# A one-core attention block: weight work moved out of the head, and a row of maxima written by eight one-column transfers

## The chip, the core and the metric

The kernel runs on one core of a Trainium2 chip. The metric is the device time of one launch in microseconds (us). Of three runs shown before the change, the median is 3070.46 us (3069.53 to 3070.96). The profile is one further execution.

## What is computed

Sixteen batches of 1024 tokens by 256 features go through an attention block and a small feed-forward block, both scaled and gated by values that come from a vector per batch. Cut to what matters here:

```
mod = silu(c) @ wmod                      # 16 x (6 * 256): sa, ca, ga, sb, cb, gb
ga, gb = sign(g) * max(|g|, 0.25)
h = layernorm(x) * (1 + ca) + sa
q = h @ Wq.T ; k, v = (h @ Wkv_down.T) @ Wk_up.T, ... @ Wv_up.T     # 8 heads of 64
x = x + ga * (softmax(q k^T / 8) v) @ Wo.T
h = layernorm(x) * (1 + cb) + sb
x = x + gb * (h @ weight.T + pooled(h) @ disha)
```

## The kernel before

All engines run one program written out by hand in slots. A slot is one batch's attention; its 64 steps are eight groups of eight. One group is half of the queries (512) of a pair of heads, so 1024 rows of scores; one step is one tile of 128 keys. Slot -1 is the head of the program: no attention yet, only what batch 0 needs. Slot 0 is batch 0's attention, and so on; the side work of the batches before and after is spread over a slot's steps.

In a step, TensorE (PE) makes the scores of one key tile in `scores()` (lines L668 and L670, two matmuls for each half), ScalarE (ACT) takes their exponential (L872), and GpSimd (POOL) adds the result to a running sum (L1043). In every fourth step PE multiplies four steps' probabilities with the values in `mix()` (L647). In every odd step `maximum()` makes plain scores for a later batch or group (L696), and VectorE (DVE) takes their maxima over the keys, negated, into two columns of `neg_max` (L1197). PE then does the step's side work (`side_work()`): projections L633, transposes L714, L729 and L769, out projection L762, feed-forward L781, sums for the denominators L748.

The maximum of each query row enters the scores as one more row of the product: row 127 of `query_m`. So a group's maxima, which DVE leaves as eight columns of 128 partitions, must be written as one row of 1024 numbers on one partition before the group's first score. The kernel before does that in three moves for each of 128 groups: PE turns the 128x8 block (L738), ACT copies the 8x128 result to `max_row` (L980), and one transfer of eight pieces of 512 bytes writes the row (L566). The first score of a group waits for it in `scores()`, at the group's step 0:

```
if k == 0:
    need(pe, max_row_set, 16 * (GROUPS * z.c + g + 1))
```

All transfers of the kernel are issued by SyncE (SP) in program order. For the group after the one under way SP issues, at steps counted in the group: copies of the queries (L558 to L560, step 1, after the last score of the group before), the spread of the denominators (four transfers L574, step 2), the reciprocals to a scratch in memory (L580, step 3), and back (two transfers L586, step 4), then the row of maxima (L566, step 6). At single steps of a slot there are also the load of the gates (L531, step 21), of the next batch (L522 and L527, steps 22 and 47), a row of ones (L547, step 30), and loads and stores of the residual.

The head (slot -1) starts with folding the weights, then normalizes and projects batch 0. The tables `FIRST` and `FOLDS` set the steps of what runs once: the gates (`gate`, L794 on PE, then `make_gates` on POOL), the columns of the second modulation (`mod_out`, the helper at L606), the transposed out weights (`wo_t`, L788), their four folds (`wo_fold`, L807) and `weight_t`. A step number of 64 or more (`STEPS + n`) means step n of slot 0. The row and the group work of batch 0 need eight queries' projections (`query`).

## Time and profile before

| | |
|---|---|
| median of three runs | 3070.46 us |
| profiled execution | 3068.32 us |
| its span in the trace | 3065.3 us |
| granted clock of TensorE, mean | 0.996 |
| PE busy | 3014.4 us, 98% of the span |
| POOL busy | 2544.3 us, 83% |
| DVE busy | 2146.2 us, 70% |
| ACT busy | 1720.2 us, 56% |
| queue of SP's transfers (q1) | 17.8% of 16 engines' span |

Busy time is the union of an engine's instructions; the profile says itself that matmuls are pipelined and that their ends are modelled, so a busy PE is not PE at its peak. The execution's own time is 3.0 us longer than its span. PE is busy in all slices of the span but the first, and the chain that ended last runs over PE for 94%.

### The profile page before, as it was taken

The page shows a single profiled execution, that of the slowest core. Times are in us where ns is not written, and L with a number is a line of the kernel's source. Part 1 is how long each engine was busy: PE and PEld are TensorE (multiplying, and loading weights), DVE is VectorE, ACT ScalarE, POOL GpSimd, SP SyncE. Part 2 cuts the span into 40 slices and gives each one's busy share as a digit, 9 for nine tenths or more (in the row PEclk, how much of TensorE's full clock was granted, in tenths as well). Part 3 has the DMA queues.
Part 4 walks back from the last instruction along what each step waited for, and adds up shares of the span by engine and source line. Part 5 has one row for each costly group of instructions (what it writes and reads, how often), then busy time and mean ns, then how long its engine had stood idle before and what let it go on. Part 6 is the DMA issues. An engine that isn't in the chain of part 4 may idle for free.

```text
span 3065.3 us, 45400 instructions
## 1 busy us (share of the span) xinstructions
PE 3014.4 (98%) x15394; PEld 1696.1 (55%) x15394; DVE 2146.2 (70%) x2548; ACT 1720.2 (56%) x3209; POOL 2544.3 (83%) x1520
## 2 busy tenths in 40 slices
PE   6999999999999999999999999999999999999998
PEld 4445555555555555555555555555555555555545
DVE  5466767767677676777767677676776767667665
ACT  3555555555555555555555555555555555555544
POOL 2788888888888888888888888888888888888796
PEclk9999999999999999999999999999999999999999
DMA  3111121121111111121211211211121111111111
GB/s 86 39 52 44 51 62 53 50 59 53 53 47 59 56 49 53 56 60 46 60 46 53 63 50 50 61 52 53 49 64 49 49 54 55 60 39 53 46 48 47
DMA packets 165621, 162.93 MB, mean 53 GB/s; under 512 B 62224, under 2 KB 113552, under 8 KB 165392
## 3 DMA queue, kind: packets, MB, share of 16 engines
q1 hardware_dynamic: 165392, 160.05, 17.8%
q8 instruction: 123, 2.02, 0.3%
q14 instruction: 106, 0.87, 0.1%
HBM read 74.40 MB, written 17.33 MB: 30 GB/s over the span
## 4 chain that ended last, share of the span: by engine, by line
PE 94%; DVE 2%; POOL 2%; DMA 1%; ACT 1%; issue 1%; SPq 0%; ACTq 0%; DVEq 0%; POOLq 0%
PE ps_mix L647 29%; PE ps_score L668 18%; PE ps_score L670 15%; PE ps_max L696 11%; PE ps_side L633 7%; PE ps_side L762 5%; PE ps_side L781 3%; PE ps_side L748 2%; POOL prob_sum L1043 1%; PE ps_side L714 1%; PE ps_side L738 1%; PE ps_side L769 1%; ACT probs L872 1%; DMA query_m<-max_row 0%; DVE neg_max L1197 0%
## 5 line engine op out<-in xcount | busy, mean ns | idle before, releaser
L1043 POOL TENSOR_TENSOR prob_sum<-prob_sum,probs 128x1024 f32<-128x1024 f32 x768 | 1861.1, 2423 | 352.8 <-ACT probs L872 275.8
L1197 DVE TENSOR_REDUCE neg_max<-ps_max 128x1 f32<-128x1024 f32 x1024 | 1204.3, 1218 | 310.9 <-PE ps_max L696 306.9
L872 ACT ACTIVATE probs<-ps_score 128x512 f32<-128x512 f32 x2048 | 1113.3, 597 | 474.0 <-PE ps_score L670 448.8
L647 PE MATMUL ps_mix<-probs,values 128*64 128x512 f32 x4096 | 935.4, 598 | 0.8 <-ACT probs L872 0.8
L668 PE MATMUL ps_score<-query,key_hi 128*128 128x512 f32 x2048 | 881.0, 430 | 9.4 <-ACT probs L872 7.9
L670 PE MATMUL ps_score<-query_m,key_lo 128*128 128x512 f32 x2048 | 809.5, 395 | 0.0
L647 PEld LDWEIGHTS ps_mix<-probs,values 128*64 128x64 f32 x4096 | 271.3, 136 | 532.8 <-issue 531.6
L668 PEld LDWEIGHTS ps_score<-query,key_hi 128*128 128x128 f32 x2048 | 384.7, 188 | 260.5 <-ACT probs L872 100.8
L670 PEld LDWEIGHTS ps_score<-query_m,key_lo 128*128 128x128 f32 x2048 | 386.7, 189 | 45.2
L696 PE MATMUL ps_max<-key_hi,query 64*128 64x512 f32 x2048 | 376.2, 445 | 3.7 <-DVE neg_max L1197 3.7
L1043 POOL TENSOR_TENSOR prob_sum<-probs 128x1024 f32<-128x1024 f32 x128 | 311.6, 2434 | 56.4 <-ACT probs L872 56.4
L909 ACT ACTIVATE mixed<-ps_mix 128x512 f32<-128x512 f32 x128 | 76.4, 597 | 327.1 <-PE ps_mix L647 327.1
L696 PEld LDWEIGHTS ps_max<-key_hi,query 64*128 64x128 f32 x2048 | 152.9, 185 | 188.5 <-issue 164.7
L980 ACT ACTIVATE max_row<-ps_side 8x128 fp32r<-8x128 f32 x127 | 33.9, 267 | 371.4 <-PE ps_side L738 371.4
L1163 DVE TENSOR_TENSOR mixed<-mixed,recip 128x512 f32<-128x512 f32 x127 | 172.2, 1356 | 97.5 <-DMA recip<-recip_scratch 96.1
L1240 DVE TENSOR_TENSOR query<-ps_side,query 64x512 fp32r<-64x512 f32 x252 | 173.6, 689 | 56.7 <-ACT query L919 52.5
L919 ACT ACTIVATE query<-ps_side 64x512 fp32r<-64x512 f32 x252 | 149.1, 592 | 78.5 <-PE ps_side L633 75.5
L1270 DVE TENSOR_TENSOR x_mid<-ps_side,x_mid 128x256 f32<-128x256 f32 x121 | 51.0, 422 | 195.2 <-PE ps_side L762 195.2
L762 PE MATMUL ps_side<-w_out_hi,mixed_lo 128*128 128x256 f32 x480 | 134.5, 280 | 0.0
L762 PE MATMUL ps_side<-w_out_lo,mixed_hi 128*128 128x256 f32 x480 | 134.5, 280 | 0.0
L762 PE MATMUL ps_side<-w_out_hi,mixed_hi 128*128 128x256 f32 x480 | 133.9, 279 | 0.0
L633 PE MATMUL ps_side<-h_hi,w_in_hi 128*128 128x512 f32 x314 | 127.1, 405 | 2.4 <-DVE query L1240 2.2
(203 smaller groups left out, 2860.0 us busy)
## 6 DMA issues: line engine op xcount, KB each, us to landing
query_m<-query SPq DMA_DIRECT2D x128, 256.0 KB, 2.5
query_m<-query SPq DMA_DIRECT2D x256, 128.0 KB, 2.6
recip<-recip_scratch SPq DMA_DIRECT2D x254, 128.0 KB, 2.9
x_in<-in_L_attn_x_dram SPq DMA_DIRECT2D x32, 512.0 KB, 4.8
x_mid<-in_L_attn_x_dram SPq DMA_DIRECT2D x64, 256.0 KB, 3.2
out_dram<-x_mid SPq DMA_DIRECT2D x64, 256.0 KB, 2.2
denoms<-recip SPq DMA_DIRECT2D x508, 1.0 KB, 1.7
gates<-gates_scratch SPq DMA_DIRECT2D x16, 256.0 KB, 4.5
```

The lines of the kernel that those rows point to most:

```text
L633: last = nc.tensor.matmul(side[:, :], w[:, f, rows], h[:, f, cols], start=(j == 0), stop=(j == len(products) - 1))
L647: last = nc.tensor.matmul(ps_mix[j * R:j * R + R, :], values[par][:, k, :], probs[:, (STEPS * z.c + s) % RING, j * HALF:(j + 1) * HALF], s ...
L668: nc.tensor.matmul(ps_score[j], key_hi[z.par][:, k * P:(k + 1) * P], group_queries(g)[:, j, :], start=True, stop=False)
L670: nc.tensor.matmul(ps_score[j], key_lo[z.par][:, k * P:(k + 1) * P], query_m[:, g % 2, j * HALF:(j + 1) * HALF], start=False, stop=True).t ...
L696: last = nc.tensor.matmul(ps_max[j][:, half * HALF:(half + 1) * HALF], query[rows, 2 * p + j, qt * P:(qt + 1) * P], key_hi[kpar][rows, hal ...
L762: last = nc.tensor.matmul(side[:, 0:D], mp[:, p, j * P:(j + 1) * P], wp[:, pair, :], start=(q == 0), stop=(q == len(products) - 1))
L872: nc.scalar.activation(probs[:, (STEPS * z.c + s) % RING, half * HALF:(half + 1) * HALF], ps_score[half], ACT.Exp, scale=SCALE).then_inc(e ...
L919: nc.scalar.activation(query[j * R:(j + 1) * R, 2 * p + j, half * HALF:(half + 1) * HALF], side[j * R:(j + 1) * R, :], ACT.Copy).then_inc( ...
L1043: nc.gpsimd.tensor_tensor(out=total[:, :], in0=before, in1=probs[:, now % RING, :], op=ALU.add).then_inc(adds_done, 1)
L1163: nc.vector.tensor_tensor(raw, raw, recip[:, :], ALU.mult).then_inc(group_mixed, 1)
L1197: nc.vector.tensor_reduce(neg_max[:, col:col + 1], ps_max[j][:, :], AX_X, ALU.max, negate=True).then_inc(maxima_done, 1)
L1240: last = nc.vector.tensor_tensor(query[(1 - j) * R:(2 - j) * R, 2 * p + j, cols], side[j * R:(j + 1) * R, :], query[j * R:(j + 1) * R, 2 * ...
```

## The change

Two parts. In the first, `wo_t`, `mod_out` and the first `wo_fold` leave slot -1 for steps 10 to 34 of slot 0, and the other folds and `weight_t` move later; the gates stay in slot -1 but are made in two halves at steps 54 and 56; one query projection goes from slot -1 to slot 0. The weights are loaded into other places so that they can live longer, and DVE takes the statistics of both halves of batch 0 before it copies the folded weights. In the second, `max_row` is gone: SP writes row 127 of `query_m` from `neg_max` itself, by eight transfers of one column of 128 numbers each, one step earlier in its program.

```
@@ tables
 FIRST = {
-    "query": (7, 58, 62, 63, STEPS, STEPS + 2, STEPS + 4, STEPS + 6),
+    "query": (7, 60, 62, STEPS, STEPS + 1, STEPS + 2, STEPS + 4, STEPS + 6),
     "values_t": (11, 12),
-    "wo_t": (54, 56),
-    "gate": (56,),
-    "max_row": (60,) + tuple(STEPS - NT + 5 + NT * i for i in range(1, GROUPS)),
-    "mod_out": (61,),
-    "wo_fold": (61, STEPS + 18, STEPS + 10, STEPS + 22),
-    "weight_t": (STEPS + 26, STEPS + 30),
+    "gate": (54, 56),
+    "mod_out": (STEPS + 10,),
+    "wo_t": (STEPS + 14, STEPS + 18),
+    "wo_fold": (STEPS + 22, STEPS + 26, STEPS + 30, STEPS + 34),
+    "weight_t": (STEPS + 36, STEPS + 38),
 }
@@ SP
-            sp.dma_start(s_wmod[:, :, 2 * D:], wmod_v[:, :, 2 * D:]).then_inc(wmod_rest_loaded, 16)
+            for j, part in enumerate((2, 5)):
+                sp.dma_start(s_wgate[:, :, j * D:(j + 1) * D], wmod_v[:, :, part * D:(part + 1) * D]).then_inc(wgate_loaded, 16)
+            sp.dma_start(s_wmod_out, wmod_v[:, :, 3 * D:5 * D]).then_inc(wmod_rest_loaded, 16)
...
-                        copy, row = STEPS + NT * (j - 1) + 1, step_of("max_row", j) + 1
+                        copy, row = STEPS + NT * (j - 1) + 1, STEPS + NT * (j - 1) + 5
...
-                            drained(sp, z, "max_row", j, need_alone)
+                            need_alone(sp, maxima_done, STEPS * b + NT * (j + 1))
                             need_alone(sp, query_m_copied, 48 * (GROUPS * b + j + 1))
-                            need_alone(sp, max_row_set, 16 * (GROUPS * b + j))
-                            sp.dma_start(query_m[P - 1:P, j % 2, :].bitcast(F32),
-                                         max_row[j % 2][:, :].bitcast(F32)).then_inc(max_row_set, 16)
+                            need_alone(sp, max_row_set, 16 * NT * (GROUPS * b + j))
+                            for u in range(NT):
+                                sp.dma_start(query_m[P - 1:P, j % 2, u * P:(u + 1) * P].bitcast(F32),
+                                             neg_max[:, NT * j + u:NT * j + u + 1].bitcast(F32),
+                                             allow_slow_non_contiguous=True).then_inc(max_row_set, 16)
@@ PE
-                        need(pe, max_row_set, 16 * (GROUPS * z.c + g + 1))
+                        need(pe, max_row_set, 16 * NT * (GROUPS * z.c + g + 1))
...
-                    elif kind == "max_row":
-                        need(pe, maxima_done, STEPS * b + NT * (i + 1))
-                        need(pe, side_drained[room], count)
-                        last = nc.tensor.transpose(side[0:NT, 0:P], neg_max[:, NT * i:NT * (i + 1)], ident[:, :])
@@ ACT
-                        elif kind == "max_row":
-                            need(act, side_full[room], count + 1)
-                            need(act, max_row_set, 16 * (GROUPS * b + i - 1))
-                            nc.scalar.activation(max_row[i % 2][:, :], side[0:NT, 0:P], ACT.Copy).then_inc(side_drained[room], 1)
@@ DVE
-            for i in range(NT // 2):
-                statistics(0, ORDER_0[0], i)
+            for part in ORDER_0:
+                for i in range(NT // 2):
+                    statistics(0, part, i)
             dve.wait_ge(fold_a, 1)
...
-            for i in range(NT // 2):
-                statistics(0, ORDER_0[1], i)
```

SP's program in the steady part, slot by slot the same. The place is slot 1, steps 26 to 33, before the change (L574, L580 and L586 carry the denominators, L566 the row of maxima, L558 to L560 the next group's queries):

```order
L574 DMA denoms<-recip 32x1x8 x4
L580 DMA recip_scratch<-denoms_r 128x8
L586 DMA recip<-recip_scratch 64x512 x2
L547 DMA key_lo<-ones_row 1x8x128
L566 DMA query_m<-max_row 1x8x128
L591 DMA out_dram<-x_mid 128x2x256
L558 DMA query_m<-query 128x512
L559 DMA query_m<-query 64x512
L560 DMA query_m<-query 64x512
```

and with the change, steps 20 to 30 of the same slot, from the reciprocals (now L591) and the load of the gates (now L534) on:

```order
L591 DMA recip<-recip_scratch 64x512 x2
L534 DMA gates<-gates_scratch 128x512
L570 DMA query_m<-neg_max 1x128x1 x8
L525 DMA x_in<-in_L0_attn_x_dram 128x4x256
L561 DMA query_m<-query 128x512
L562 DMA query_m<-query 64x512
L563 DMA query_m<-query 64x512
L579 DMA denoms<-recip 32x1x8 x4
L585 DMA recip_scratch<-denoms_r 128x8
L591 DMA recip<-recip_scratch 64x512 x2
L570 DMA query_m<-neg_max 1x128x1 x8
L550 DMA key_lo<-ones_row 1x8x128
```

Where one transfer stood, eight stand; the load of the next batch and the row of ones, which stood ahead of the row, now stand behind it, and the load of the gates still stands ahead.

PE's program in the head, from the first group's scores for maxima on (L696; the first group's are the first four sets), before:

```order
L696 MATMUL ps_max<-key_hi,query 128x512 x4
L788 MATMUL ps_mix<-ident,probs 128x128 x4
L696 MATMUL ps_max<-key_hi,query 128x512 x4
L788 MATMUL ps_score<-ident,probs 128x128 x4
L794 MATMUL ps_score<-probs,mixed 16x256 x4
L696 MATMUL ps_max<-key_hi,query 128x512 x4
L633 MATMUL ps_side<-h_hi,w_in_hi 128x512
```

and, after that query's projection (L633), the end of the first group's maxima:

```order
L696 MATMUL ps_max<-key_hi,query 128x512 x4
L738 MATMUL ps_mix<-ident,neg_max 8x128
L696 MATMUL ps_max<-key_hi,query 128x512 x4
L606 MATMUL ps_score<-mixed,probs 128x16 x8
L807 MATMUL ps_score<-mixed 64x256 x2
```

With the change, from the same place to the first projection (L701 is the old L696, L795 the old L794, L638 the old L633):

```order
L701 MATMUL ps_max<-key_hi,query 128x512 x4
L795 MATMUL ps_mix<-probs,mixed 16x256 x2
L701 MATMUL ps_max<-key_hi,query 128x512 x4
L795 MATMUL ps_score<-probs,mixed 16x256 x2
L701 MATMUL ps_max<-key_hi,query 128x512 x8
L638 MATMUL ps_score<-h_hi,w_in_hi 128x512
```

Between the first group's four sets of scores only the two halves of the gates are left, and the query's projection stands behind all four; the transposes, the modulation (L606) and the fold (L807) are gone from the head.

## Rows read from the trace of the kernel before

**Rows 1.** The page: the chain that ended last, shares by engine.

```profile
PE 94%; DVE 2%; POOL 2%; DMA 1%; ACT 1%; issue 1%; SPq 0%; ACTq 0%; DVEq 0%; POOLq 0%
```

**Rows 2.** Timeline, 1512 to 1528 us: start, duration, engine, line, operation, count.

```profile
1512.50 2.46 SPq L574 DMA_DIRECT2D denoms<-recip  x4
...
1516.10 2.36 DVE L1197 TENSOR_REDUCE neg_max<-ps_max 128x1 f32<-128x1024 f32 x2 [0.90 <-PE ps_max L696]
...
1520.14 1.14 SPq L586 DMA_DIRECT2D recip<-recip_scratch  x2
...
1524.41 0.72 SPq L566 DMA_DIRECT2D query_m<-max_row  x1
...
1527.80 0.50 PE L668 MATMUL ps_score<-query,key_hi 128*128 128x512 f32 x1
```

**Rows 3.** Timeline of SP and PE, two later groups, 1591 to 1620 us.

```profile
1591.30 1.13 SPq L586 DMA_DIRECT2D recip<-recip_scratch  x2
...
1598.14 0.50 PE L668 MATMUL ps_score<-query,key_hi 128*128 128x512 f32 x1
...
1614.28 0.52 SPq L531 DMA_DIRECT2D gates<-gates_scratch  x1
...
1619.95 0.50 PE L668 MATMUL ps_score<-query,key_hi 128*128 128x512 f32 x1
```

**Rows 4.** Timeline of SP, one of the late groups, 752 to 761 us.

```profile
756.04 1.13 SPq L586 DMA_DIRECT2D recip<-recip_scratch  x2
...
760.52 0.53 SPq L558 DMA_DIRECT2D query_m<-query  x1
```

**Rows 5.** Sources: single instructions, ns min/median/max, first and last start.

```profile
L738 PE MATMUL ps_side<-ident,neg_max x127: 272/273/273, 79.7 to 3005.4; 128*8 128x128 f32 x127
...
L574 SPq DMA_DIRECT2D denoms<-recip x508: 523/591/1683, 98.7 to 3018.6; - x170
...
L558 SPq DMA_DIRECT2D query_m<-query x128: 492/516/545, 34.9 to 2987.1; - x128
...
L566 SPq DMA_DIRECT2D query_m<-max_row x128: 670/720/744, 49.8 to 3006.1; - x128
...
L515 SPq DMA_DIRECT2D gates_scratch<-x_mid x4: 412/420/424, 81.2 to 82.6; - x4
```

**Rows 6.** The page: issues by line, KB each, median us from issue to landing.

```profile
query_m<-query SPq DMA_DIRECT2D x128, 256.0 KB, 2.5
...
denoms<-recip SPq DMA_DIRECT2D x508, 1.0 KB, 1.7
...
gates_scratch<-x_mid SPq DMA_DIRECT2D x4, 8.0 KB, 1.4
mixed<-in_L_c_dram SPq DMA_DIRECT2D x2, 8.0 KB, 3.4
```

**Rows 7.** Timeline of PE, end of a `mix()`: with L738 behind it.

```profile
1499.27 1.89 PE L647 MATMUL ps_mix<-probs,values 128*64 128x512 f32 x8
1501.09 0.27 PE L738 MATMUL ps_side<-ident,neg_max 128*8 128x128 f32 x1
...
1501.43 0.40 PE L670 MATMUL ps_score<-query_m,key_lo 128*128 128x512 f32 x1
```

**Rows 8.** The same in the last batch, where no L738 stands.

```profile
3023.81 1.89 PE L647 MATMUL ps_mix<-probs,values 128*64 128x512 f32 x8
...
3025.97 0.40 PE L670 MATMUL ps_score<-query_m,key_lo 128*128 128x512 f32 x1
```

**Rows 9.** Timeline of PE and POOL in the head and slot 0; brackets: idle before, what ended it.

```profile
24.67 1.97 PE L714 MATMUL ps_score<-ident,x_in 128*128 128x128 f32 x8 [4.27 <-POOL x_in L1011]
...
34.29 0.65 PE L788 MATMUL ps_mix<-ident,probs 128*128 128x128 f32 x4
...
38.15 3.46 PE L794 MATMUL ps_score<-probs,mixed 128*16 128x256 f32 x8
...
50.42 3.59 PE L606 MATMUL ps_score<-mixed,probs 128*128 128x16 f32 x16
...
53.95 1.97 PE L807 MATMUL ps_score<-mixed 64*64 64x256 f32 x4
...
60.76 0.39 PE L668 MATMUL ps_score<-query,key_hi 128*128 128x512 f32 x1
...
71.64 0.24 POOL L997 TENSOR_SCALAR rstd<-moments 128x4 f32<-128x4 f32 x1 [20.78 <-DVE moments L1112]
...
97.12 1.08 PE L748 MATMUL ps_side<-prob_sum,ones_cols 128*32 128x256 f32 x8 [3.88 <-POOL prob_sum L1043]
```

**Rows 10.** Windows: us, busy (x count) of PE, PEld, DVE, ACT, POOL, granted clock, DMA share, GB/s.

```profile
50.00:60.00 10.00, 10.00 (x37) 7.00 (x34) 2.71 (x5) 1.77 (x3) 0.86 (x3) 0.58 0.18 53
```

More of the change, by code:

```diff
@@ L306, in adaln_block @@
         query_m = sb("query_m", [P, 2, T], F32R)
-        neg_max = sb("neg_max", [P, STEPS])
-        max_row = [sb(f"max_row{i}", [NT, P], F32R) for i in range(2)]
+        neg_max = sb("neg_max", [P, STEPS], F32R)
         probs = sb("probs", [P, RING, T])
@@ L341, in adaln_block @@
         s_disha = stage[1][:, 2304:2560]
[L342 to L344 removed]
+        s_c = stage[1][:, 5120:5120 + NF * B].rearrange("p (k b) -> p k b", k=NF)
+        s_silu = stage[1][:, 5152:5152 + 3 * NF * B].rearrange("p (j k b) -> p j k b", j=3, k=NF)
+        s_wo_t = stage[1][:, 3712:4736].rearrange("p (k n) -> p k n", k=PAIRS)
         s_w_in = probs[:, 0:2, 0:H * R + P]
@@ L419, in adaln_block @@
         wmod_rest_loaded = sem("wmod_rest_loaded")
+        wgate_loaded = sem("wgate_loaded")
         qk_loaded = sem("qk_loaded")
@@ L599, in _, with modulate @@
         def _(pe):
-            def modulate(bank, parts):
-                for j, part in enumerate(parts):
+            def modulate(bank, weight):
+                for j, part in enumerate((1, 0)):
                     for f in range(NF):
@@ L606, in modulate @@
                             last = nc.tensor.matmul(bank[:, (2 * j + f) * B:(2 * j + f + 1) * B],
-                                                    s_wmod[:, k, part * D + f * P:part * D + (f + 1) * P],
+                                                    weight[:, k, part * D + f * P:part * D + (f + 1) * P],
                                                     s_silu[:, 2, k, :], start=(k == 0), stop=(k == NF - 1))
@@ L789, in side_work @@
                     elif kind == "gate":
-                        pe.wait_ge(wmod_rest_loaded, 16)
+                        if i == 0:
+                            pe.wait_ge(wgate_loaded, 32)
                         need(pe, side_drained[room], count)
-                        for j, part in enumerate((2, 5)):
-                            for k in range(NF):
-                                last = nc.tensor.matmul(side[0:B, j * D:(j + 1) * D], s_silu[:, 2, k, :],
-                                                        s_wmod[:, k, part * D:(part + 1) * D], start=(k == 0), stop=(k == NF - 1))
+                        for k in range(NF):
+                            last = nc.tensor.matmul(side[0:B, 0:D], s_silu[:, 2, k, :], s_wgate[:, k, i * D:(i + 1) * D],
+                                                    start=(k == 0), stop=(k == NF - 1))
                     elif kind == "mod_out":
                         pe.wait_ge(side_drained[room], count)
-                        last = modulate(side, (4, 3))
+                        pe.wait_ge(wmod_rest_loaded, 16)
+                        last = modulate(side, s_wmod_out)
                     elif kind == "wo_fold":
@@ L967, in slot @@
                             need(act, side_full[room], count + 1)
-                            nc.scalar.activation(s_gate[2], side[0:B, :].rearrange("p (j n) -> p j n", j=2),
-                                                 ACT.Copy).then_inc(side_drained[room], 1)
+                            nc.scalar.activation(s_gate[2][:, i, :], side[0:B, 0:D], ACT.Copy).then_inc(side_drained[room], 1)
                         elif kind == "wo_fold":
@@ L1016, in make_gates @@
                 sign, size, raw = s_gate[0], s_gate[1], s_gate[2]
-                drained(pool, z, "gate", 0, need_alone)
+                for i in range(2):
+                    drained(pool, z, "gate", i, need_alone)
                 nc.gpsimd.tensor_scalar(sign, raw, 0.0, 2.0, ALU.is_ge, ALU.mult).then_inc(gate_steps, 1)
```

18 lines of the change are left out of this document (8 added, 10 removed).

## The prediction

> **What bounds the kernel now.** I read the chain of the page first, then the timeline around one group boundary, then SP's part of it over a batch, then the head. The chain runs over PE for 94% [rows 1], and the page has PE busy in every slice but the first: in slots 1 to 15 whatever delays PE is paid in full, and whatever another engine saves is worth nothing by itself. POOL, busy 83%, does not stop PE there. So three questions decide: what the removed transposes cost PE, whether the new transfers deliver the row of maxima before PE asks for it, and what the head gives.
>
> The reader should see in [rows 2] how late the row of maxima is made. SP's last duty before it is the pair of transfers L586, issued by 1520.14 + 1.14 = 1521.28. The group's maxima were complete at 1516.10 + 2.36 = 1518.46. The first score of the next group starts at 1527.80. I call the time between, 6.52 us, the window: the whole row must be issued and landed in it, because the new code lets SP go on as soon as the maxima are there, without waiting for PE and ACT. Before the change SP sat idle to 1524.41, issued once for 0.72, and the row was in time.
>
> **Part by part.**
>
> *The windows.* They repeat slot by slot, because both of their ends hang on PE's own fixed order. Groups of four places in a slot of eight have about 6.5 us. Three places have 5.7: 1591.30 + 1.13 = 1592.43 to 1598.14 [rows 3]. The place with the load of the gates has less, since that load still stands ahead of the row: 1614.28 + 0.52 = 1614.80 to 1619.95, 5.15 us. The load of the next batch and the row of ones, which shorten two places before, move behind the row and cost it nothing. In about 20 of the 126 groups of the steady part something came late, mostly the store of reciprocals; one of them is 756.04 + 1.13 = 757.17, the next group's copies starting at 760.52 just before its first score at about 761.0, a window of 3.8 [rows 4].
>
> *What the row needs.* Eight issues one after another and the landing of the last: about 0.1 to start, 7 times the distance of two issues, and one landing. No element-wise transfer inside the memory of the core is in the trace, so both are bounded by neighbours. The distance: L515 takes 0.42 to issue, which with a gap of 0.04 gives 0.46; L558, also 128 partitions, takes 0.516; L566, the old row, takes 0.72 [rows 5]. The nearest in kind is L574: small, inside the core's memory, between one partition and many, issued in a loop. Four of them take 2.46 [rows 2], the last 0.59, so a distance of (2.46 - 0.59) / 3 = 0.62. I take 0.62, with 0.46 and 0.76 as ends. The landing: 1.4 for L515, 1.7 for L574, 2.5 for the copies of queries, 3.4 for the load of `c`, which also goes number by number [rows 6]. I take 1.7, again L574's. Need: 0.1 + 7 x 0.62 + 1.7 = 6.14 us; ends 0.1 + 7 x 0.46 + 1.4 = 4.7 and 0.1 + 7 x 0.76 + 2.5 = 7.9.
>
> Why not the old row's 0.72, whose destination is the same partition? It has eight pieces and the new ones have 128 each, the count of L558, which is issued faster. The Trainium skill, DMA: Bandwidth & Descriptors, section "Why a DMA increments its semaphore by 16 and not by 1", says that a transfer whose slowest dimension is 8 uses 8 engines and SP then writes the missing increments itself, while 128 uses all 16. By that rule the 0.72 holds an extra that the new ones don't pay; with 0.76 as the distance instead, the sum below would be about 105 us higher.
>
> *What is missing is a stall of PE.* At a need of 6.14: the places with 6.5 stay free; some 37 regular groups with 5.7 lose 0.43 each, 16 us; some 14 with 5.15 lose 1.0, 14 us; about 21 late or odd groups lose 1.3 on average, 27 us. Sum **+57 us**. PE can't win this back: it is busy throughout and everything behind moves with it. The ends of the need give about +5 and, with a mean window of 5.85, 126 x 2.1 = +265.
>
> *The transposes.* 127 of L738 at 0.272 would be 34 us [rows 5], but they hide. With L738 between, L670 starts 0.27 after the end of the last `mix()` matmul (1501.43 against 1499.27 + 1.89) [rows 7]; in the last batch, where nothing stands between, also 0.27 (3025.97 against 3023.81 + 1.89) [rows 8]. The small matmul runs in the time in which PE changes from one tiling to the other. I take -1 us, with -34 as the far end. ACT's copy and its wait go too; ACT is no bound, and its exponentials wait for PE's scores anyway: nothing.
>
> *The head.* Two savings. The second half's statistics now run before the copies, so POOL normalizes it earlier; PE's idle 4.27 before L714 at 24.67 [rows 9] shrinks, ACT's chain behind it starts about 3 us earlier. Then the gates hold up the third set of scores for maxima in one piece of 3.46; the halves now fit into PE's waits for DVE. L788 (0.65, twice), L606 (3.59), L807 (1.97) and one projection (about 2.5 there) leave PE before the first score. That comes at 60.76 and should come near 49, then set by DVE's maxima and the row's transfers. POOL's next work waits for DVE's statistics of the next batch at 71.64 and paces PE to 97.12; both follow the first score, so about 11 us is won there. Given back in slot 0, where PE is the bound again after about 105: the transposes, the fold and part of the modulation, some 3 us at full clock; PE will also be idler in the head, and its granted clock, a mean of 0.58 between 50 and 60 us before (much of it at the lower level, 1.2 GHz) [rows 10], may cost part of the gain. I take **-8 us**, between -3 and -12. The loads have more issues (one more on SP ahead of the first row) and land long before steps 54 and 74: nothing. The later fold reaches POOL's gating at step 35 within a step of its wait; POOL has slack there and its ring of six steps covers PE: nothing, 2.5 at worst, once.
>
> *Sum.* The profiled execution took 3068.3: 3068.3 + 57 - 1 - 8 = 3116.3. The median of the runs shown lies 2.1 above it, so I forecast **3118 us**.
>
> **The rivals.**
>
> *The row fits.* If two issues lie 0.46 apart and land in 1.4, the need is 4.7 and only a handful of late groups stall, 5 us or less; what is left is the head. For it: SP is idle for 3 us in every window, and the new code starts earlier on purpose; single issues as short as 0.42 exist. Against it: none of the more than 1000 issues inside the core's memory is that short in the median. It decides below a need of about 5.1: 3070.5 - 1 - 8 + 3 = 3064, on the edge of what can be told, and if the transposes were on PE's path after all (against [rows 7, 8]) 3070.5 - 34 - 8 = 3028. This is the case on the other side of mine.
>
> *Numbers one by one are slow.* Each transfer writes 128 numbers of 4 bytes into one partition. The load of `c` is the only such pattern here and needs 3.4 to land [rows 6]. With 3.4 for 1.7 the need is 7.8, the stall 126 x 2.0 = 250, the time about 3310. For it: all 128 writes meet in one partition. Against it: that load has 2048 numbers per transfer, sixteen times as many, and comes from outside. The Trainium skill, DMA: Bandwidth & Descriptors, section "Rules for kernel authors", says not to transpose by a plain copy with a rearranged pattern and gives a factor of 19; it would make this rival the outcome. It speaks of bulk rate, and here 4 KB move in a window of microseconds, so I give it little.
>
> *The issue is as slow as the old row's.* With 0.76 apart and 1.7, the need is 7.1, and all places stall: 126 x (7.1 - 5.85), near 155, plus a little for the late groups, 3225.
>
> **How the numbers follow.** My forecast, a need between about 5.5 and 6.9, has 0.68 and gives 3082 to 3195. The row that fits has 0.19; of it 0.12 ends below 3064, 0.07 around 3067. Slow numbers 0.06, slow issues 0.07. The range reaches from 3066 to 3200: it leaves out the better part of the fitting row and the two slow cases, about 2 in 10. Faster or slower by 0.2% is about what a measurement of this kernel can tell from no change, 6 us: faster 0.12, within 0.08, slower 0.80.
>
> **What would show it.** In the profile after: eight issues per group on SP, 0.55 to 0.65 apart, starting right behind L586's successor instead of 3 us later; PE idle before the first score of a group, released by the transfer `query_m<-neg_max`, for some 60 to 80 of 128 groups, longest behind the load of the gates and zero at four places of the slot; PE's busy time lower by 34 but its span not; the first score near 49 us and the first denominators near 86. I would be wrong if that wait is absent (then distance or landing is shorter than any neighbour's), if it stands before all groups (then longer), or if PE's time from the last `mix()` to L670 falls by more than 0.05 per group.

## The result, and the profile after

The changed kernel takes **3241.03 us** (median of 4 runs, 3232.63 to 3255.41), the kernel before in the same sitting 3069.99: a ratio of 1.056, 95% interval 1.054 to 1.0579. It is slower by 171 us. I had forecast slower, but by 48 us, and the result lies above my range. The profiled execution took 3247.02 us, its span is 3245.2 (before 3065.3), its mean granted clock 0.983 (before 0.996).

The chain of the page, which ran over PE for 94% before [rows 1], now runs over PE for half; the rest is the row and what surrounds it. Page of the changed kernel, chain by engine and by line (L570 is the row, L673 and L675 the scores, L591 the reciprocals back, L585 their store):

```profile
PE 52%; SPq 19%; DMA 13%; issue 7%; DVE 6%; ACT 2%; POOL 1%; ACTq 0%; DVEq 0%; POOLq 0%
SPq L570 15%; PE ps_mix L652 15%; PE ps_score L673 11%; PE ps_score L675 8%; DMA query_m<-neg_max 7%; PE ps_max L701 6%; DMA recip_scratch<-denoms_r 5%; DVE neg_max L1191 5%; PE ps_side L638 4%; SPq L591 4%; PE ps_side L763 3%; PE ps_side L749 2%; PE ps_side L782 1%; POOL prob_sum L1039 1%; ACT probs L874 1%
```

Busy time on the page, and the two waits for the row (waits by engine and line: total, times, longest):

```profile
PE 3052.8 (94%) x15266; PEld 1720.0 (53%) x15266; DVE 2135.3 (66%) x2548; ACT 1688.6 (52%) x3082; POOL 2537.4 (78%) x1520
```

```profile
PE ps_score L673 <- DMA query_m<-neg_max: 143.7, 106, 3.2
...
PEld ps_score L673 <- DMA query_m<-neg_max: 200.1, 126, 3.6
...
DVE mixed L1157 <- DMA recip<-recip_scratch: 178.1, 111, 4.5
```

So the 179.9 us by which the span grew are two things. PE idles 3245.2 - 3052.8 = 192.4 us where it idled 50.9 before: +141.5. The waits for the row alone are 143.7 (PE itself waits in 106 of the 128 groups; its weight load, which stands ahead of the matmul, in 126). And PE is busy 38.4 us **more** (3052.8 against 3014.4), with 128 matmuls fewer. The granted clock says why. The lower level, 1.2 GHz, is half of the full one, so a mean of 0.983 means that (1 - 0.983) x 2 x 3245.2 = 110 us of the span ran at it.

One group, the place with the load of the gates; timeline of SP's queue and of PE in the changed kernel, answering [rows 3]:

```profile
1500.93 1.13 SPq L591 DMA_DIRECT2D recip<-recip_scratch  x2
1502.16 0.52 SPq L534 DMA_DIRECT2D gates<-gates_scratch  x1
1502.89 5.03 SPq L570 DMA_DIRECT2D query_m<-neg_max  x8
1508.07 0.48 SPq L525 DMA_DIRECT2D x_in<-in_L_attn_x_dram  x1
```

```profile
1509.39 0.80 PE L673 MATMUL ps_score<-query,key_hi 128*128 128x512 f32 x1 [2.99 <-DMA query_m<-neg_max]
...
1509.98 0.63 PE L675 MATMUL ps_score<-query_m,key_lo 128*128 128x512 f32 x1
...
1510.41 0.63 PE L673 MATMUL ps_score<-query,key_hi 128*128 128x512 f32 x1
```

The need can be read off whole. By the need I mean, as in the prediction, the time from the end of SP's last duty to the score. From 1502.16 + 0.52 = 1502.68 to 1509.39 are 6.71 us: 0.21 to the first issue, seven distances of (5.03 - 0.60) / 7 = 0.633, together 4.43 (0.60 is the median issue below), and 2.07 from the last issue to the score. The last part is 2.08 in the median of all groups that wait. Source and issues of the row, answering [rows 5] and [rows 6]:

```profile
L570 SPq DMA_DIRECT2D query_m<-neg_max x1024: 469/601/1661, 43.6 to 3187.0; - x171
```

```profile
query_m<-neg_max SPq DMA_DIRECT2D x1024, 0.5 KB, 2.2
...
denoms<-recip SPq DMA_DIRECT2D x508, 1.0 KB, 1.7
```

The same rows of PE show the second loss: after the idle 2.99 a score matmul takes 0.63 where it otherwise takes 0.40 [rows 7], and the first scores of the two halves start 1.02 apart (1509.39 and 1510.41). Windows of the changed kernel over that place (us, busy of PE, PEld, DVE, ACT, POOL, granted clock, DMA share, GB/s):

```profile
1502.00:1509.00 7.00, 4.40 (x26) 3.13 (x24) 4.27 (x7) 2.17 (x4) 6.57 (x4) 1.00 0.32 76
1509.50:1512.50 3.00, 3.00 (x7) 2.37 (x8) 1.35 (x2) 1.19 (x2) 0.73 (x1) 0.50 0.82 272
1513.00:1519.00 6.00, 6.00 (x35) 2.33 (x33) 2.95 (x3) 2.34 (x5) 2.36 (x1) 1.00 0.10 25
```

The clock falls to half behind the idle stretch, and PE does seven matmuls in 3 us, where at one each 0.23 us (1501.67, 1501.90 and 1502.13 in the kernel before) some thirteen fit. The span has 28 stretches at the lower level, against 4 before. Of the 28, 25 begin during or just after one of the 106 waits for the row: none at the 57 waits below 1.2 us, 25 at the 49 longer ones.

The next group shows the late kind, answering [rows 4] (timeline of SP and PE):

```profile
1526.01 0.33 SPq L585 DMA_DIRECT2D recip_scratch<-denoms_r  x1
...
1529.26 1.12 SPq L591 DMA_DIRECT2D recip<-recip_scratch  x2
...
1530.60 5.03 SPq L570 DMA_DIRECT2D query_m<-neg_max  x8
...
1537.10 0.50 PE L673 MATMUL ps_score<-query,key_hi 128*128 128x512 f32 x1 [1.92 <-DMA query_m<-neg_max]
```

SP may issue the reciprocals' way back (L591) only when their store (L585) has landed. From the one issue to the other are 3.25 us here and 1.47 in the median. I call a store late where it is over 2.5: that is so in 21 groups of the changed kernel and in 9 of the kernel before (counted over the trace). These 21 groups carry 50.6 us of the wait. In 16 others one of the eight issues of the row is slow (up to 1.66 us for 0.60), so that the last one starts more than 4.8 us behind the first instead of 4.43; they carry 19.2, and the remaining groups 73.9.

In the head the first score comes at 51.80 instead of 60.76 [rows 9].

### The profile page after: what moved, and what is told of

Read it like the earlier page. It is cut to its first block, busy times and chain, and to the rows that moved or that the text cites. A ratio compares the mean times of both kernels' runs of the same rounds, so it can differ in the third digit from the quotient of the medians.

```text
span 3245.2 us, 45663 instructions
## 1 busy us (share of the span) xinstructions
PE 3052.8 (94%) x15266; PEld 1720.0 (53%) x15266; DVE 2135.3 (66%) x2548; ACT 1688.6 (52%) x3082; POOL 2537.4 (78%) x1520
## 3 DMA queue, kind: packets, MB, share of 16 engines
q1 hardware_dynamic: 311344, 160.11, 19.2%
## 4 chain that ended last, share of the span: by engine, by line
PE 52%; SPq 19%; DMA 13%; issue 7%; DVE 6%; ACT 2%; POOL 1%; ACTq 0%; DVEq 0%; POOLq 0%
SPq L570 15%; PE ps_mix L652 15%; PE ps_score L673 11%; PE ps_score L675 8%; DMA query_m<-neg_max 7%; PE ps_max L701 6%; DMA recip_scratch<-denoms_r 5%; DVE neg_max L1191 5%; PE ps_side L638 4%; SPq L591 4%; PE ps_side L763 3%; PE ps_side L749 2%; PE ps_side L782 1%; POOL prob_sum L1039 1%; ACT probs L874 1%
## 5 line engine op out<-in xcount | busy, mean ns | idle before, releaser
L1191 DVE TENSOR_REDUCE neg_max<-ps_max 128x1 fp32r<-128x1024 f32 x1024 | 1204.1, 1217 | 326.9 <-PE ps_max L701 322.7
L673 PE MATMUL ps_score<-query,key_hi 128*128 128x512 f32 x2048 | 895.8, 437 | 151.7 <-DMA query_m<-neg_max 143.7
L675 PE MATMUL ps_score<-query_m,key_lo 128*128 128x512 f32 x2048 | 820.5, 401 | 0.0
L673 PEld LDWEIGHTS ps_score<-query,key_hi 128*128 128x128 f32 x2048 | 390.2, 191 | 511.5 <-DMA query_m<-neg_max 200.1
L1039 POOL TENSOR_TENSOR prob_sum<-probs 128x1024 f32<-128x1024 f32 x128 | 303.7, 2373 | 182.0 <-ACT probs L874 182.0
L675 PEld LDWEIGHTS ps_score<-query_m,key_lo 128*128 128x128 f32 x2048 | 393.1, 192 | 47.2
L701 PE MATMUL ps_max<-key_hi,query 64*128 64x512 f32 x2048 | 379.0, 448 | 8.9 <-DVE neg_max L1191 6.2
L701 PEld LDWEIGHTS ps_max<-key_hi,query 64*128 64x128 f32 x2048 | 154.4, 187 | 196.8 <-issue 180.4
L1264 DVE TENSOR_TENSOR x_mid<-ps_side,x_mid 128x256 f32<-128x256 f32 x121 | 50.9, 421 | 200.3 <-PE ps_side L763 200.3
L638 PE MATMUL ps_side<-h_hi,w_in_hi 128*128 128x512 f32 x314 | 132.8, 423 | 6.2 <-DVE query L1234 6.2
L638 PE MATMUL ps_side<-h_lo,w_in_hi 128*128 128x512 f32 x314 | 130.2, 415 | 0.0
```

Source lines behind the costliest of these rows:

```text
L638: last = nc.tensor.matmul(side[:, :], w[:, f, rows], h[:, f, cols], start=(j == 0), stop=(j == len(products) - 1))
L673: nc.tensor.matmul(ps_score[j], key_hi[z.par][:, k * P:(k + 1) * P], group_queries(g)[:, j, :], start=True, stop=False)
L675: nc.tensor.matmul(ps_score[j], key_lo[z.par][:, k * P:(k + 1) * P], query_m[:, g % 2, j * HALF:(j + 1) * HALF], start=False, stop=True).t ...
L701: last = nc.tensor.matmul(ps_max[j][:, half * HALF:(half + 1) * HALF], query[rows, 2 * p + j, qt * P:(qt + 1) * P], key_hi[kpar][rows, hal ...
L1039: nc.gpsimd.tensor_tensor(out=total[:, :], in0=before, in1=probs[:, now % RING, :], op=ALU.add).then_inc(adds_done, 1)
L1191: nc.vector.tensor_reduce(neg_max[:, col:col + 1], ps_max[j][:, :], AX_X, ALU.max, negate=True).then_inc(maxima_done, 1)
```

## The experiments

Each kernel was timed against the kernel before on the same chip. I call them e1 to e11, in the order in which they stand here.

### The head part alone

The changed tables, loads and statistics order, with the row as before:

```
-                            for u in range(NT):
-                                sp.dma_start(query_m[P - 1:P, j % 2, u * P:(u + 1) * P].bitcast(F32),
...
+                            sp.dma_start(query_m[P - 1:P, j % 2, :].bitcast(F32),
+                                         max_row[j % 2][:, :].bitcast(F32)).then_inc(max_row_set, 16)
```

> The first part of the change alone: gates, modulation and fold of the weights moved, statistics first; the row of maxima goes by transpose, copy and one transfer as before. Theory (the head is a gain, and the whole loss is PE waiting for the row): 3070 - 8 = 3062 us, between 3058 and 3067; PE's idle time before a group's first score stays below 3 us in all. Rival A (the work moved into slot 0, or the earlier start, is part of the loss): above 3075 us.

Measured: **3063.69 us** (10 runs, 3061.02 to 3068.4) against 3067.99; ratio 0.9987 (0.9978 to 0.9996). A gain of 4 us, about half of the 8 that I had in the sum. Timeline of PE, the first score and the first denominators, answering [rows 9]:

```profile
51.58 0.52 PE L674 MATMUL ps_score<-query,key_hi 128*128 128x512 f32 x1
...
92.82 0.64 PE L754 MATMUL ps_side<-prob_sum,ones_cols 128*32 128x256 f32 x8 [1.32 <-POOL prob_sum L1050]
```

The first score is 9.2 us earlier, the first denominators only 97.12 - 92.82 = 4.3, and that is what the span keeps (3060.8 against 3065.3). PE waits 3.6 us in all for the row, a little over the 3 that I had allowed.

### The row part alone

The same lines the other way round, in the kernel before: its tables and loads, with the eight transfers.

> The second part alone: eight transfers of one column for the row, the head as before. Theory: the changed kernel's 3241 plus the 8 us of the head that is not won: 3240 to 3260 us, PE's idle time before first scores about 145 us, the granted clock's mean about 0.98. Rival A: clearly below 3240, by what the head part would cost.

Measured: **3247.05 us** (3242.36 to 3256.78), ratio 1.0587 (1.0566 to 1.0607), clock 0.983. PE waits 147.9 us for the row. As expected: the whole loss is the row.

### Six of the eight columns at step 3

```
-                        if s == row % STEPS and there:
+                        if s in ((row - 2) % STEPS, row % STEPS) and there:
+                            early = s == (row - 2) % STEPS
...
-                            for u in range(NT):
+                            for u in (0, 1, 2, 4, 5, 6) if early else (3, 7):
```

> The changed kernel, but six of the eight columns, whose maxima are done two steps before, are sent between the spread of the denominators and the store of the reciprocals, where SP was idle; only two transfers are left behind the reciprocals' way back. Same number of transfers, same numbers, one order. Theory (the row's last issue and landing end after the window): the need falls from 0.2 + 7 x 0.63 + 2.1 = 6.7 to 0.2 + 0.63 + 2.1 = 2.9 us, less than any regular window, so the waits vanish and with them the low clock: 3061 us, between 3057 and 3072. Rival B (1024 transfers of single numbers slow the memory or the queue as such): still above 3150.

Measured: **3138.29 us** (3129.88 to 3141.64), ratio 1.0232 (1.0215 to 1.0249); the clock is 0.997. A miss: 60% of the loss goes, and a new wait comes. SP's queue in the timeline, and the waits of PE and DVE:

```profile
1516.67 2.49 SPq L580 DMA_DIRECT2D denoms<-recip  x4
1519.37 4.90 SPq L571 DMA_DIRECT2D query_m<-neg_max  x6
1524.42 0.49 SPq L586 DMA_DIRECT2D recip_scratch<-denoms_r  x1
1526.05 1.15 SPq L592 DMA_DIRECT2D recip<-recip_scratch  x2
1527.30 1.18 SPq L571 DMA_DIRECT2D query_m<-neg_max  x2
```

```profile
PE ps_max L702 <- DVE neg_max L1192: 52.7, 44, 2.5
PE ps_score L674 <- DMA query_m<-neg_max: 11.3, 20, 1.8
```

```profile
DVE mixed L1158 <- DMA recip<-recip_scratch: 310.0, 127, 6.3
```

The wait for the row fell from 143.7 to 11.3, so the row is in time when only two columns are late. But the six stand ahead of the store of the reciprocals (L586). They come back late, DVE waits 310 us for them instead of 96, its next maxima wait behind that on the same engine, and PE waits for DVE. What I had left out was the queue behind the inserted issues.

### The transpose issued twice, in the kernel before

```
+                        for _ in range(2):
-                        last = nc.tensor.transpose(side[0:NT, 0:P], neg_max[:, NT * i:NT * (i + 1)], ident[:, :])
+                            last = nc.tensor.transpose(side[0:NT, 0:P], neg_max[:, NT * i:NT * (i + 1)], ident[:, :])
```

> The kernel before with each of the 128 transposes of the maxima issued twice into the same place. Theory (the transpose hides in PE's change of tiling, so its removal gave nothing): if it is hidden wholly, the second adds at most its own 0.1 to 0.2 us where the first already fills the gap: 3070 to 3095 us, and the time from the last mix matmul to L670 shows how much of the first was hidden. Rival C (each transpose costs its 0.27 us): 3070 + 34 = 3104 us.

Measured: **3086.52 us** (3082.67 to 3089.6), ratio 1.0059 (1.0044 to 1.0074): by the ratio 18 us (14 to 23) for 128 more matmuls, 0.14 each. In the traces the score matmul L670 starts 0.976 us behind the start of the last `mix()` matmul, and 0.866 in the kernel before: 0.11 each. This doesn't say by itself what the first one costs; e9 does.

### PE kept busy in front of the wait

```
+                    if k == 0 and (z.c or g):
+                        need(pe, exps_done, 2 * (STEPS * z.c + s) - 1)
+                        for _ in range((1, 1, 3, 6, 1, 3, 3, 1)[g]):
+                            nc.tensor.matmul(ps_score[0], key_hi[z.par][:, k * P:(k + 1) * P],
+                                             group_queries(g)[:, 0, :], start=True, stop=True)
                     if k == 0:
```

> The changed kernel, with matmuls whose result is thrown away put in front of PE's wait for the row at every group's first score: 1, 1, 3, 6, 1, 3, 3, 1 of them by place in the slot, 0.4 us each, 19 in a slot, about as long as the median gap of each place in the changed kernel (0.34, 0.16, 0.96, 1.71, 0.30, 0.94, 0.95, 0.43). They add 19 x 0.4 x 16 = 122 us of PE's work, of which some 95 us stand in time that PE waited anyway. Theory A, TensorE's clock falls because PE sits idle at the group starts and that costs (110 - 30) / 2 = 40 us: the granted clock returns from 0.983 to 0.993 or more, PE's idle falls from 145 us to below 80, and the median is 3241 - 40 + 25 = 3226 (3205 to 3240). Rival B, the clock falls for another reason (the removed transposes, the transfers): the clock stays at 0.983 and the median is 3241 + 25 = 3266 (3250 to 3275).

Measured: **3221.1 us** (3212.89 to 3225.19), ratio 1.0496 (1.0475 to 1.0518), clock 0.993. PE does some 300 useless matmuls more than the changed kernel and is done 20 us sooner. That is theory A; rival B would be 3266. Its wait for the row is down from 143.7 to 50.2, and (1 - 0.993) x 2 x 3211.1 = 45 us are left at the lower clock instead of 110, a gain of 32. Not all of the time won need be the clock's: this trace has 14 late stores where the changed kernel has 21. What shows the cause is the granted clock itself, which rival B left at 0.983.

### The wait behind one more matmul

The second half's first product, which doesn't read the row, is issued before the wait instead of behind it; the two `key_lo` products follow together.

```
+                        if k > 0 or j == 1:
+                            if k == 0:
+                                need(pe, max_row_set, 16 * NT * (GROUPS * z.c + g + 1))
+                            for i in (0, 1) if k == 0 else (j,):
+                                nc.tensor.matmul(ps_score[i], key_lo[z.par][:, k * P:(k + 1) * P],
```

> The changed kernel, with PE's wait for the row moved behind the second half's first matmul at a group's first step, so that two matmuls that don't read the row (0.4 to 0.5 us) come before the wait instead of one. Theory A, the row arrives a fixed time after SP's last duty before it (0.21 + 7 x 0.633 + 2.07 = 6.71 us) and PE's wait is all that it costs: every place's gap shrinks by 0.47 us or to zero, (0.34 + 0.16 + 0.47 + 0.47 + 0.30 + 0.47 + 0.47 + 0.43) x 16 = 50 us of stall, and with it 10 to 20 us of low clock: 3241 - 65 = 3176 (3160 to 3195). ACT gets the first half's scores 0.4 us later, which costs nothing as long as PE is the bound. Rival B, the first half's scores set ACT and PE's next step waits for ACT: what is won before the wait is lost at the next step, 3230 to 3245.

Measured: **3190.84 us** (3186.51 to 3197.02), ratio 1.0395 (1.0373 to 1.0417), clock 0.992. Inside the range of theory A. The wait, now at L675, is down by 59 us:

```profile
PE ps_score L675 <- DMA query_m<-neg_max: 84.4, 85, 3.1
```

### Four of the eight columns at step 2

As with the six, but:

```
-                            early = s == (row - 2) % STEPS
-                            need_alone(sp, maxima_done, STEPS * b + NT * (j + 1) - 2 * early)
-                            for u in (0, 1, 2, 4, 5, 6) if early else (3, 7):
+                            early = s == (row - 3) % STEPS
+                            need_alone(sp, maxima_done, STEPS * b + NT * (j + 1) - 4 * early)
+                            for u in (0, 1, 4, 5) if early else (2, 3, 6, 7):
```

> The changed kernel, with the row in two halves: four columns, whose maxima are complete by then, at the group's step 2 ahead of the spread of the denominators, where SP has been idle for 8 us (1510.7 to 1519.8 in the changed kernel's trace); the other four where all eight stood. Theory A (row need = 0.21 + 3 x 0.633 + 2.07 = 4.2 us, below even the 5.15 of the shortest regular place, and the early four fill an idle stretch of SP, so the store of reciprocals isn't delayed as with six at step 3): PE's idle at group starts falls from 145 to below 20 us, the wait for recip stays near the 96 us of the kernel before, the clock is 0.995 or more, and the median is that of the head part alone, 3064 (3058 to 3080). Rival B, more small transfers disturb the other transfers wherever they stand: DVE's wait for recip grows to over 200 us and the median is 3100 to 3150. Rival C, the wait of SP for the copies' landing at step 2 delays the spread itself: 3080 to 3120, with the spread behind the four by less than 0.1 us.

Measured: **3084.14 us** (3083.94 to 3085.71), ratio 1.0047 (1.0031 to 1.0062), clock 0.996. Nine tenths of the loss are gone with the same 1024 transfers, in the same shape, on the same queue. SP's queue in the timeline, and two waits:

```profile
1513.41 2.44 SPq L571 DMA_DIRECT2D query_m<-neg_max  x4
1517.55 2.49 SPq L580 DMA_DIRECT2D denoms<-recip  x4
1523.74 0.33 SPq L586 DMA_DIRECT2D recip_scratch<-denoms_r  x1
```

```profile
PE ps_max L702 <- DVE neg_max L1192: 19.0, 17, 2.5
...
PE ps_score L674 <- DMA query_m<-neg_max: 6.9, 11, 2.0
```

```profile
DVE mixed L1158 <- DMA recip<-recip_scratch: 193.5, 114, 4.3
```

The row is in time, as the need of 4.2 us says. The median is 4 us above theory A's range, and 20 above the head part alone: DVE still waits for the reciprocals twice as long as before (193.5 against 96.1, near the 200 of rival B, whose time did not come), 21 groups have a late store as in the changed kernel, and PE waits 19.0 for DVE's maxima instead of 3.7. Rival C falls, since 1.7 us lie between the four and the spread. The small transfers are not what makes the stores late: e9 below has none of them and 22 late stores, 20 of them at the same groups as in the changed kernel. They come with the rest of the second part (no transpose and no copy, the row a step earlier, other places of the tiles in memory); which of these it is stays open, as no run takes them apart.

### Half of the columns on ACT's queue

```
+                                for u in (4 + 2 * i, 5 + 2 * i):
+                                    act.dma_start(query_m[P - 1:P, j % 2, u * P:(u + 1) * P].bitcast(F32),
```

> The changed kernel, with four of the eight columns issued by ACT instead of SP: two after its exponentials of step 5, two after those of step 6. Theory A (issues one after another on one queue make the row late): SP's half needs 0.21 + 3 x 0.633 + 2.07 = 4.2 us; ACT's last two are issued by about 2.5 us before the group's first score and land as it comes, a gap of at most 0.5; ACT is busy 57% and the 1.3 us of each pair delay its exponentials by less than its slack. PE's idle at group starts falls below 50 us and the median is 3064 to 3110. Rival B, ACT's exponentials come late behind the issues and PE waits for them: PE's waits for exps and ACT's chain grow, 3110 to 3200. Rival C, two queues share the engines and each transfer takes longer to issue: distance over 0.8 us, stalls as before, over 3200.

Measured: **3217.32 us** (3210.7 to 3224.57), ratio 1.048 (1.0456 to 1.0504), clock 0.981. A miss for A and not B either; the time is that of rival C. Issues of the page, and the timeline of one group:

```profile
query_m<-neg_max SPq DMA_DIRECT2D x512, 0.5 KB, 2.7
query_m<-neg_max ACTq DMA_DIRECT2D x512, 0.5 KB, 2.1
```

```profile
1505.17 2.47 SPq L570 DMA_DIRECT2D query_m<-neg_max  x4
1505.47 1.18 ACTq L885 DMA_DIRECT2D query_m<-neg_max  x2
...
1511.33 0.80 PE L673 MATMUL ps_score<-query,key_hi 128*128 128x512 f32 x1 [3.09 <-DMA query_m<-neg_max]
```

ACT was 52% busy in the changed kernel, not 57%. The median distance of two issues is 0.64 on SP and 0.51 on ACT (rival C's 0.8 is wrong), but here the last issue starts at 1507.05 and the score comes 4.3 us later instead of 2.07. The stall has moved to three places of the slot, with medians of 2.31, 0.99 and 3.09, while the other five have none; from the last issue to the score are 4.5, 3.2 and 4.5 us at the three in the median. Two queues nearly halve the issuing, and the landing gives it back there: in kind what rival C feared, two queues in each other's way, though not by the issues. What at those places delays it (this one has the load of the gates just ahead) stays open.

### A row that costs nothing

```
-                            for u in range(NT):
-                                sp.dma_start(query_m[P - 1:P, j % 2, u * P:(u + 1) * P].bitcast(F32),
...
+                            sp.dma_start(query_m[P - 1:P, j % 2, :].bitcast(F32),
+                                         ones_row[:, :].bitcast(F32)).then_inc(max_row_set, 16)
```

> The kernel before, with PE's transpose of the maxima, ACT's copy and their waits taken out, and the row written by one transfer of eight pieces of 512 bytes as before, but from a constant tile of ones, issued at step 5 when the maxima are complete. The maxima are still taken but not used; the exponential's scale is divided by 16 so that it stays finite, which its time doesn't depend on. So this is the row part with a transfer that costs nothing: what the removed transposes are worth alone. Theory A (the small matmul runs while PE changes from one tiling to the other, 0.27 us from mix() to the next score with it and without): no gain, 3063 to 3071. Rival B (127 transposes of 0.272 stand on PE's path): 3070 - 34 = 3036 (3030 to 3042). Between, a gain of 0.06 per transpose, would be 3060.

Measured: **3073.24 us** (10 runs, 3069.73 to 3077.73) against 3071.5; ratio 1.0008 (0.9999 to 1.0017). Taking all 128 transposes away gains nothing. PE's busy time is 3014.6, with them 3014.4. The run is not quite alike otherwise: it has 22 late stores instead of 9, and two waits grew, from 96.1 and 3.7:

```profile
DVE mixed L1151 <- DMA recip<-recip_scratch: 133.3, 89, 4.6
...
PE ps_max L693 <- DVE neg_max L1185: 13.8, 11, 3.6
```

These 10 us of PE could hide a gain of that size in the median. The timeline of PE rules it out, answering [rows 7] (L644 is `mix()`, L665 and L667 the scores):

```profile
1503.60 3.65 PE L644 MATMUL ps_mix<-probs,values 128*64 128x512 f32 x16
1507.18 0.50 PE L665 MATMUL ps_score<-query,key_hi 128*128 128x512 f32 x1
1507.53 0.40 PE L667 MATMUL ps_score<-query_m,key_lo 128*128 128x512 f32 x1
```

From the start of the last `mix()` matmul to the start of L667 are 0.861 us in the median here and 0.866 with the transpose between: 0.005 each, under 1 us in all.

### The order of the statistics alone

In the kernel before, on DVE ahead of the copies of the folded weights:

```
-            for i in range(NT // 2):
-                statistics(0, ORDER_0[0], i)
+            for part in ORDER_0:
+                for i in range(NT // 2):
+                    statistics(0, part, i)
```

> The kernel before, with one piece of the head part alone: DVE takes the statistics of both halves of batch 0 before it copies the folded weights. The trace of the kernel before has PE idle for 4.27 us before the transposes at 24.67, of which 1.5 was left in the kernel with the head part alone. Theory A: the head part's small gain (the span 4.5 us shorter) comes mostly from this, 2 to 3 us: 3067 (3064 to 3069). Rival B: it comes from the work that leaves PE before the first score, and this piece alone gives under 1 us, 3069 to 3071.

Measured: **3068.02 us** (10 runs, 3065.97 to 3068.92) against 3071.5; ratio 0.9988 (0.9979 to 0.9997). By the medians 3.5 us, the size of the head part's 4.3. Its first denominators:

```profile
93.53 0.64 PE L748 MATMUL ps_side<-prob_sum,ones_cols 128*32 128x256 f32 x8 [2.43 <-POOL prob_sum L1043]
```

They are 3.6 us earlier than before, and only 0.7 us behind the head part's, although the first score here comes at 57.78, 6.2 us behind the head part's.

### The head part with the late wait

The first and the sixth edit together.

> The head part alone, with PE's wait for the row behind the second half's first matmul as well. In the kernel with the head part alone PE waits for the row only 4 times, 3.6 us in all, each wait over 0.47, so at most 2 us are to be had. Theory: 3062 (3060 to 3066), the same as the head part alone within what can be measured and 0.1 to 0.3% under the kernel before. Rival: the first half's scores come 0.4 us later at every group start, ACT's exponentials with them, and 128 x some 0.1 are lost: 3070 or more.

Measured: **3073.82 us** (11 runs, 3070.7 to 3074.44) against 3071.5; ratio 1.0006 (0.9997 to 1.0015). No gain: what the later wait won in e6 it does not win where nothing has to be waited for, and the head part's 4 us are lost. The time is that of the rival, but its reason is not shown: PE's wait for ACT's exponentials is 8.0 us against 6.4, while PE is 7.8 us busier with the same number of matmuls (3017.9 against 3010.1). What makes it busier is open. The head part alone and the order of the statistics alone (e10) are the two versions that lie clear below the kernel before, both by about 0.1%.

## Why the prediction was wrong

*What bounds the kernel: right.* PE was the bound everywhere in the steady part, and the window from SP's last duty to the next group's first score decided. The order of the places was as forecast: the median wait is 1.71 us at the one with the load of the gates, 0.94 to 0.96 at the three with 5.7, 0.16 to 0.43 at the four with 6.5. My sum was also right as a sum: over the 127 windows of the kernel before, group by group, a need of 6.14 gives 56 us.

*The distance of two issues: right.* 0.633 against 0.62, from the four issues of the spread. The Trainium skill, DMA: Bandwidth & Descriptors, section "Rules for kernel authors", warns off transposing by a plain copy with a factor of 19. At this size no such factor shows: one column of 128 numbers is issued in 0.60, less than the old row's 0.72.

*The landing: the step that failed.* I took 1.7 from the spread. The page has 2.2, and from the last issue to the score pass 2.07. With 0.21 instead of 0.1 for the start and 0.09 more for the distances the need is 6.71 and not 6.14. The difference of 0.57 us looks small, but the four places with 6.5 lie between the two values: I had them free, and now nearly all groups are on the wrong side. A wait before all groups was the sign that I had named for a longer need. The same windows of the kernel before give 106 us at 6.71 instead of 56, and from there on each tenth of a microsecond of need costs some 12 us more. This was a cliff at 6.5, and I gave a forecast as if a few tenths were noise. e7 confirms the need from the other side: four columns need 4.2, and the wait is nearly gone.

*The windows taken over unchanged: a second part of it.* Those 50 us alone would have left the forecast at 3168, inside my range. The wait measured is 143.7, and the other 37 us are windows and issues that the change made worse. The 21 groups with a late store lose 2.4 us each, where I had 1.3 for 21 late or odd groups, and 16 more groups have a slow issue of the row. I had also read the trace of before wrongly there: of 21 short windows only 9, not most, have a late store.

*The clock: the term that was missing.* I weighed the granted clock only for the head and put it at nothing in the steady part, without a reason. But each wait is idle time of PE, and at 25 of the 106, all of them of 1.2 us and more, the clock falls to 1.2 GHz. The 110 us at the lower clock, less the 25 of before by the same reckoning, cost half of their difference, 42 us, and the busy time shows 38. e5 supports it: with PE kept busy the clock comes back, and the time falls although work was added. The Trainium skill, TensorE: Matmul & The Clock Gate, section "HAM oscillation — how this bites in real kernels", describes a kernel that waits for a transfer before each tile and starts each tile at the lower clock. This trace agrees in kind, but here 25 stretches follow on 106 waits, not one on each.

*The transposes: right.* I took -1 instead of -34, because from the end of `mix()` to L670 were 0.27 with and without one [rows 7, 8]. I wrote that nothing else stands between; the matmul L668 does, in both cases (1501.12 and 3025.63), so the comparison holds. e9 takes all of them out, and L670 then starts 0.005 us earlier each time. Only the sign that I gave, a busy time lower by 34, was wrong: without them it is 3014.6, with them 3014.4.

*The head: right in sign, twice too large.* -8 in the sum, -4 measured. The first score came 9 us earlier (I had near 12), but I held that the first denominators follow the first score. They don't: they hang on POOL, and POOL on DVE's statistics. They came 4.3 earlier (e1). By e10 the order of the statistics alone gives nearly all of it; the work taken out of PE's head gives at most a microsecond or two more, within what the intervals leave open.

*The sum, rebuilt:* +57 as forecast, +50 for the need, +37 for the rest of the measured wait (late stores, slow issues and what else shortened the windows), +38 of clock, -4 for the head make 178; the span grew by 179.9.

*The rivals.* None happened as written. "The issue is as slow as the old row's" came near in the number (3225) with a need of 7.1, but by luck: its mechanism, 0.76 between issues, is not there. "Numbers one by one are slow" had the right term, the landing, at 3.4 instead of 2.07. "The row fits" needed less than 5.1.

## What to carry to other kernels

Before a wait on the engine that bounds is replaced by transfers, compare need and window place by place, and treat a need within half a microsecond of a window as undecided: the loss is paid in each of the 128 groups. A bounding TensorE that starts to wait can also pay at the clock: here 38 us on top of 142 of idle time, with falls only at waits of 1.2 us and more. And a chain of small transfers should be split into the stretches in which its queue is idle: the same 1024 transfers cost 171 us all behind the last duty, 70 with six of eight ahead of a store that others wait for, and 15 with four of eight in an idle stretch (all three with the head part's gain of 4 in them).

## What the runs showed of the hardware

- One column of 128 numbers of 4 bytes, from 128 partitions into one, takes 0.60 us to issue on SP, 0.633 from issue to issue, and 2.07 from the last issue to the matmul that waits for it. The spread, of 1 KB between one partition and 32, lands in 1.7.
- A 128x8 transpose between two tilings of PE costs nothing that can be measured: the score behind it starts 0.005 us later, and taking all out gives a ratio of 1.0008 (e9, 0.9999 to 1.0017). A second one behind it costs 0.11 us in the trace, 0.14 by the medians.
- In the middle of a kernel that is otherwise busy the clock fell to 1.2 GHz behind 25 of 49 idle stretches of 1.2 to 3.2 us, and behind none of 57 shorter ones; which of the long ones, the traces here don't settle.
- Issuing from two queues at once leaves the distance of issues at 0.64 on SP and gives 0.51 on ACT, but at three of eight places the wait from the last issue to the score is 3.2 to 4.5 us instead of 2.07.
- A store of 4 KB to memory, which otherwise lets the next transfer start after 1.47 us, took over 2.5 us (up to 3.8) in 8 or 9 of 127 cases where the row went by transpose and copy, and in 14 to 25 in the others, with small transfers or without; the cause is open.
